# A recurrent and windowed-attention network on one core: another order of work around the exponentials, zero rows stored in turns, gated weights loaded in parts

## The reference, cut to what matters

```
h = shift_token(x)                       # second half of the columns from the token before
q, k, v = split(h @ wqkv)                # 8 heads of 64
q, k = rotary_xpos(l2norm(q) * qs, l2norm(k) * ksc)
o = softmax(mask(8 * q @ k.T)) @ v       # windows of 128 tokens, each sees itself and the one before
x = x + o @ wo
h = layernorm(shift_token(x)) * lg + lb
a, g = split(h @ w1 + b1)                # 2 x 682
x = x + (a * gelu(g)) @ w2 + b2
```

## Time and profile before

| | |
|---|---|
| median of 3 runs | 6583.36 us |
| the profiled execution | 6587.74 us, its span 6585.7 us |
| TensorE matmul | 5333.4 us busy (81%) |
| VectorE | 4306.0 us (65%) |
| GpSimd | 3300.1 us (50%) |
| ScalarE | 2826.9 us (43%) |
| first attention | about 1899 to 3103 us of the span |
| first gated stage | about 3103 to 3709 us |
| second attention | about 3709 to 4889 us |
| second gated stage | about 4889 to 5495 us |

### The profile page before, as it was taken

One profiled execution on the slowest core, in us unless ns is written; L12 is line 12 of the kernel. 1 busy time (PEld: TensorE's weight loads), 2 busy tenths in 40 slices (PEclk: granted clock), 3 DMA queues, 4 the chain that ended last, 5 costly groups with the idle time before them and its releaser, 6 DMA issues. The chain is left out here.

```text
span 6585.7 us, 79275 instructions
## 1 busy us (share of the span) xinstructions
PE 5333.4 (81%) x26028; PEld 3102.2 (47%) x26028; DVE 4306.0 (65%) x8780; ACT 2826.9 (43%) x6006; POOL 3300.1 (50%) x1922
## 2 busy tenths in 40 slices
PE   6777777777648888887999888888869998996878
PEld 2222222222226666665555466666645554554755
DVE  5999999999956666665333366666643334663349
ACT  5776767767624444443111244444431112331233
POOL 5989898999944334442001233443320103776424
PEclk8888888788769999998999999999989999998988
DMA  5555555555530111111111110011111114443856
GB/s 121 128 126 128 120 129 122 137 119 131 120 107 30 33 30 30 30 31 41 44 39 48 44 32 30 30 30 33 30 40 48 39 45 153 131 135 85 224 172 196
DMA packets 501100, 549.85 MB, mean 83 GB/s; under 512 B 71749, under 2 KB 401349, under 8 KB 496596
## 3 DMA queue, kind: packets, MB, share of 16 engines
q1 hardware_dynamic: 463460, 522.79, 29.2%
q10 hardware_dynamic: 9584, 19.80, 0.9%
q0 software_dynamic: 27648, 2.19, 0.4%
HBM read 395.60 MB, written 218.35 MB: 93 GB/s over the span
## 5 line engine op out<-in xcount | busy, mean ns | idle before, releaser
L616 POOL TENSOR_TENSOR db<-durep,brep 128x2048 f32<-128x2048 f32 x256 | 1159.8, 4531 | 176.1 <-DVE p_h L523 161.3
L1089 POOL TENSOR_TENSOR rn<-n,mhalf 128x16 f32<-128x16 f32 x128 | 374.9, 2929 | 1311.2 <-DVE n L1047 1311.2
L466 ACT ACTIVATE p_h<-dlrep,am 128x512 f32<-128x512 f32 x1024 | 703.9, 691 | 205.4 <-DVE hh L534 169.3
L321 PE MATMUL p_acc<-hh,fold 128*32 128x512 f32 x2048 | 355.2, 773 | 487.2 <-DVE hh L534 486.8
L523 DVE TENSOR_TENSOR_SCAN p_h<-p_h,hlast,db 128x512 f32<-128x512 f32 x576 | 720.7, 1284 | 0.0
L1324 POOL TENSOR_TENSOR grstd<-grstd,mhalf 128x4 f32<-128x4 f32 x32 | 32.6, 1018 | 1065.2 <-DVE grstd L1272 1065.2
L1257 ACT ACTIVATE gg<-p_g,b 114x512 f32<-114x512 f32 x192 | 132.0, 687 | 975.0 <-PE p_a L1223 974.9
L534 DVE TENSOR_TENSOR hh<-p_h,crep 128x512 f32<-128x512 f32 x768 | 520.0, 677 | 0.0
L800 PE MATMUL p_qk<-wqkv,hT 128*128 128x512 f32 x1024 | 502.6, 614 | 8.1 <-DVE rot_sin L1041 7.2
L927 ACT ACTIVATE probB<-probB,nb 128x256 f32<-128x256 f32 x512 | 253.6, 496 | 549.5 <-DVE nb L1006 549.5
L1790 POOL DMA_INDIRECT dispatched<-xe,idx x384 | 395.3, 1029 | 130.7 <-issue 113.8
(11 more groups left out here) (251 smaller groups left out, 11845.6 us busy)
## 6 DMA issues: line engine op xcount, KB each, us to landing
dlrep<-delta_rows SPq DMA_DIRECT2D x256, 256.0 KB
durep<-drive_rows SPq DMA_DIRECT2D x256, 256.0 KB
ew<-in_L_ffn_w SPq DMA_DIRECT2D x192, 176.0 KB
brep<-bc_rows SPq DMA_DIRECT2D x64, 256.0 KB
crep<-bc_rows SPq DMA_DIRECT2D x64, 256.0 KB
delta_rows<-dl SPq DMA_DIRECT2D x64, 256.0 KB
drive_rows<-du SPq DMA_DIRECT2D x64, 256.0 KB
hx<-stream SPq DMA_DIRECT2D x256, 64.0 KB, 2.0
```

The source lines that it names most:

```text
L321: ins = pe.matmul(p_acc[32 * j:32 * j + 32, :], fold[:], hh[s % 2][:, j], start=False, stop=(g == NG - 1), skip_group_check=True)
L466: act.activation(p_h[:, (i % BANKS) * CH:(i % BANKS + 1) * CH], dlrep[use % 2][:, j], ACT.Exp, scale=am[:, q, j, g:g + 1]).then_inc(s_ex, 1)
L616: pool.tensor_tensor(out=db[s % 2][:], in0=durep[use % 2][:], in1=brep[c % 2][:, g:g + 1, :].to_broadcast([P, 4, CH]), op=ALU.mult).then_i ...
L1089: pool.tensor_tensor(out=rn[k][:], in0=n2[k][:], in1=mhalf[:], op=ALU.pow).then_inc(s_rn, 1)
```

## The change

In attention:

- TensorE's order becomes: scores A, turned input, weighted values B, scores B, project, queries/keys 1, and on as before.
- ScalarE's order becomes: turned B, turned input, exps A 1 and 2, output, exps A 3 and 4, turned A, 4 exps B, squares, and on as before.
- VectorE takes the maxima of B right after the division of A, ahead of the residual.
- Each of the four maxima gives a signal of its own, and each exponential waits for its own one.
- The 16 stores of zero rows are issued one in every fourth round of the first layer, at the round's head.

In the gated stage SP loads the first activations, then `w1` in two halves, the second activations, and `w2`. ScalarE's queue loads scale and shift, `b1` and `b2`. Each load has a semaphore of its own group, and an engine waits for it at its first use.

```diff
@@ attention, TensorE: scores
-                        pe.wait_ge(s_nb[1], t)
+                        pe.wait_ge(s_nb[1], 4 * t)
                 else:
-                    pe.wait_ge(s_nb[0], t + 1)
+                    pe.wait_ge(s_nb[0], 4 * (t + 1))
@@ attention, TensorE: the round
                     scores(t, 0)
-                if t >= 1:
-                    weighted_values(t - 1, 1)
                 if f < NT:
                     turn_in(f)
                 if t >= 1:
-                    project(t - 1)
+                    weighted_values(t - 1, 1)
                 if now:
                     scores(t, 1)
+                if t >= 1:
+                    project(t - 1)
@@ attention, ScalarE: exps
-            def exps(t, half):
-                if t > 1:
+            def exps(t, half, js):
+                if js[0] == 0 and t > 1:
                     act.wait_ge(s_rden[half], t - 1)
-                act.wait_ge(s_nb[half], t + 1)
-                for j in range(4):
+                for j in js:
                     h = head_at(half, j)
+                    act.wait_ge(s_nb[half], 4 * t + j + 1)
                     ins = act.activation(prob[half][:, j], prob[half][:, j], ACT.Exp, bias=nb[:, h:h + 1], scale=-1.0,
                                          accum_out=den[t % 2][:, h:h + 1])
-                ins.then_inc(s_exp[half], 1)
+                if js[-1] == 3:
+                    ins.then_inc(s_exp[half], 1)
@@ attention, ScalarE: the round
+                if l == 0 and now and t % (NT // NZ) == 0:
+                    clear_slots(t // (NT // NZ))
                 if t >= 1:
                     turn_prob(t - 1, 1)
-                    turn_out(t - 1)
                 if f < NT:
                     turn_in(f)
                 if now:
-                    exps(t, 0)
-                    exps(t, 1)
+                    exps(t, 0, (0, 1))
+                if t >= 1:
+                    turn_out(t - 1)
+                if now:
+                    exps(t, 0, (2, 3))
                     turn_prob(t, 0)
+                    exps(t, 1, (0, 1, 2, 3))
@@ attention, VectorE: maxima, then the round
-                ins.then_inc(s_nb[half], 1)
+                    ins.then_inc(s_nb[half], 1)
...
                     normalise(t, 0)
+                    maxima(t, 1)
                 if t >= 1:
                     residual(t - 1)
                 if now:
-                    maxima(t, 1)
@@ gated, SP
-            sp.dma_start(w1[:], A["L0_ffn_w1"][l].rearrange("(c p) n -> p c n", p=P)).then_inc(s_w, 16)
...
+            load_h(0)
+            for f in range(DH):
+                sp.dma_start(w1[:, f], A["L0_ffn_w1"][l, f * P:(f + 1) * P, :]).then_inc(s_w1l, 16)
+            load_h(1)
             for j in range(NJ):
                 n = BLK[j]
-                sp.dma_start(w2[0:n, j, :], A["L0_ffn_w2"][l, j * BJ:j * BJ + n, :]).then_inc(s_w, 16)
...
+                sp.dma_start(w2[0:n, j, :], A["L0_ffn_w2"][l, j * BJ:j * BJ + n, :]).then_inc(s_w2l, 16)
@@ gated, ScalarE
-            act.wait_ge(s_w, 16 * GLOADS)
+            for q, nm in enumerate(("L0_ffn_ln_g", "L0_ffn_ln_b")):
+                v = A[nm][l].unsqueeze(1)
+                for f in range(DH):
+                    act.dma_start(lgb[:, q, f:f + 1], v[f * P:(f + 1) * P, :]).then_inc(s_ln, 16)
+            b1f = A["L0_ffn_b1"][l].unsqueeze(1)
+            for j in range(NJ):
+                for q in (1, 0):
+                    n, at = BLK[j], q * HID + j * BJ
+                    act.dma_start(b1[0:n, q, j:j + 1], b1f[at:at + n, :]).then_inc(s_b1l, 16)
+            act.dma_start(b2[:], A["L0_ffn_b2"][l:l + 1, :].to_broadcast([P, D])).then_inc(s_b2l, 16)
+            act.wait_ge(s_b1l, 32 * NJ)
```

More of the change, by code:

```diff
@@ L955, in values, with clear_slots @@
                 act.activation(vv[f % RING][:], p_v[:], ACT.Copy).then_inc(s_ve, 1)
[L957 to L961, removed]
+            def clear_slots(n):
+                if n == 0:
+                    act.wait_ge(s_zeros, 1)
+                act.dma_start(xb_d[n * ZR * P:(n + 1) * ZR * P, :].rearrange("(p r) e -> p (r e)", r=ZR),
+                              slot_zeros[:]).then_inc(s_zeroed, 16)
             for t in range(-2, NT + 1):
                 now, f = 0 <= t < NT, t + 2
+                if l == 0 and now and t % (NT // NZ) == 0:
+                    clear_slots(t // (NT // NZ))
                 if t >= 1:
                     turn_prob(t - 1, 1)
-                    turn_out(t - 1)
                 if f < NT:
@@ L1092, in _ @@
                 if f >= RING:
-                    pool.wait_ge(s_nb[1], f - RING + 1)
+                    pool.wait_ge(s_nb[1], 4 * (f - RING + 1))
                 pool.wait_ge(s_rn, f + 1)
@@ L1159, in gated @@
     p_y = ps("p_y", CT * D)
-    s_w = sem("g_weights")
+    s_w1l, s_w2l, s_b1l, s_ln, s_b2l = (sem("g_" + n) for n in ("w1_loads", "w2_loads", "b1_loads", "ln_loads", "b2_load"))
     s_h, s_r, s_out = ([sem(f"g_{n}{k}") for k in range(2)] for n in ("h", "r", "out"))
@@ L1175, in load_h @@
                                  tiles(rows(2 * l + 1, chunk_slot(c), CH, src)[:, cols])).then_inc(s_h[c % 2], 16)
-            sp.dma_start(w1[:], A["L0_ffn_w1"][l].rearrange("(c p) n -> p c n", p=P)).then_inc(s_w, 16)
-            b1f = A["L0_ffn_b1"][l].unsqueeze(1)
+            load_h(0)
+            for f in range(DH):
+                sp.dma_start(w1[:, f], A["L0_ffn_w1"][l, f * P:(f + 1) * P, :]).then_inc(s_w1l, 16)
+            load_h(1)
             for j in range(NJ):
                 n = BLK[j]
-                sp.dma_start(w2[0:n, j, :], A["L0_ffn_w2"][l, j * BJ:j * BJ + n, :]).then_inc(s_w, 16)
[L1182 to L1191, removed]
+                sp.dma_start(w2[0:n, j, :], A["L0_ffn_w2"][l, j * BJ:j * BJ + n, :]).then_inc(s_w2l, 16)
             for c in range(NC):
@@ L1217, in up @@
                 if j == 0:
+                    if c == 0:
+                        pe.wait_ge(s_w1l, 16 * DH)
                     pe.wait_ge(s_hT, c + 1)
@@ L1227, in down @@
             def down(c):
+                if c == 0:
+                    pe.wait_ge(s_w2l, 16 * NJ)
                 pe.wait_ge(s_hid, NJ * (c + 1))
@@ L1237, in down @@
                     ins.then_inc(s_w2, 1)
-            pe.wait_ge(s_w, 16 * GLOADS)
             turn(0)
@@ L1303, in residual @@
                                   op=ALU.add).then_inc(s_y, 1)
-            dve.wait_ge(s_w, 16 * GLOADS)
             prepare(0)
+            dve.wait_ge(s_ln, 32 * DH)
             turn(0)
+            dve.wait_ge(s_b1l, 32 * NJ)
             for c in range(NC):
@@ L1324, in rsqrt @@
                 pool.tensor_tensor(out=rstd[:], in0=rstd[:], in1=mhalf[:, 0:CT], op=ALU.pow).then_inc(s_rs, 1)
-            pool.wait_ge(s_w, 16 * GLOADS)
             rsqrt(0)
+            pool.wait_ge(s_b2l, 16)
             for c in range(NC):
@@ L1333, in _ @@
                                    op=ALU.add).then_inc(s_rb, 1)
-GLOADS = 1 + 3 * NJ + 2 * DH + 1
 def route(nc, ctx, A, rows, x_in, ssm_out, xb_d, x1_d, xn1_d, xt_d, y_d, odd_d, kv_d, ident, mhalf, zrow):
```

## The result

The changed kernel takes 6308.44 us (median of 4 runs, 6303.65 to 6311.38), the one before 6584.01: a ratio of 0.958, 95% interval 0.9564 to 0.9597. Forecast were 6315 and a range of 6278 to 6410.

A forecast was written before the change was run, and what follows sets the result against it. TensorE was the nearest bound, with holes from waits. Gains of 220 (tiles), 23 (zero rows) and 25 (gated loads) sum to 268 us: 6319.7 from the profiled 6587.7, 6315 against the median; range 6278 to 6410.

The forecast's parts named there:

- The wait before the turning of queries and keys: TensorE in attention: 1.57 us a tile waiting for ScalarE's copy of the turned probabilities, forecast to go.
- The division A as what is late next: VectorE in attention: division A, running against GpSimd, ends 6.97 us after the power, at 8.07; the turning of A follows.
- The period: Attention tile: from 17.85 to 16.11 us, steady gain 1.75 us in 126 tiles, 220 us.
- The last tile of each layer: Attention: the gain needs a full neighbouring tile, so 63 of a layer's 64 tiles were counted.
- The signals, priced at nothing: Attention: signals on each maximum and waits on each exponential cost 0, upper end 0.4 us a tile or 50 us.
- The second rival: Attention: division A's last quarter also waits for GpSimd's table product; period 16.85, gain 126 us, time 6409; chance 0.14.
- Zero rows: Start of the first attention: without sixteen stores ahead of the loads, first scores come 22.8 us sooner; spread stores are hidden.
- Gated loads: Start of both gated stages: activations loaded before weights move the chain forward 12.5 us each, 25 in all.
- by the division and by TensorE's own queue alike: TensorE in attention: the turning of A starts at 8.17 us after the scores A, held by both.
- the first rival: Attention: TensorE alone decides, small waits vanish; period 15.9 to 15.8, gain 252 us, time 6283; chance 0.12.
- The slower rival: Attention: division A waits for GpSimd and its four parts hold GpSimd back; period 19.0, time 6679; chance 0.05.
- the one in which only the beginnings gain: Attention: all four division parts wait until GpSimd is through; loop stays 17.85, time 6535; chance 0.05.

The follow-up runs named there:

- the first experiment: Kernel before with one edit, ScalarE copying the turned A ahead of the exponentials B: 6488.7 us, ratio 0.9857.
- the second: Kernel before with only TensorE's order changed (turned input, weighted values B, scores B, projection): 6589.1 us, ratio 1.001.
- two experiments: Kernel after with one signal for four maxima, 6381.0 us; kernel before with only the turned A ahead of the exponentials B, 6488.7 us.
- the extra product: Kernel after with one more GpSimd product (1.04 us, into a scratch tile) between power and sum of each tile: 6451.0 us, ratio 0.9802.
- the experiment: Kernel after, but four maxima give one signal and an exponential waits for all four of its half: 6381.0 us, ratio 0.9694.
- the two experiments with the norms first: Kernel after with norms ahead of VectorE's rotation products, 6250.5 us; that kernel with exponentials B ahead of the turned A again, 6230.6 us.

## Why the prediction was right, step by step

- **The wait before the turning of queries and keys** goes because ScalarE copies the turned A first: shown by the first experiment, where it is gone, and by the second, where it stays.
- **The division A as what is late next, its end read from the second layer's first tile** (6.97 us after the power): 6.98 in the timeline after. The same pattern of collisions came back with the same start, 4.13 against 4.10; where the start was later, 5.10 and 5.39 in two experiments, the end was later too, 7.57 and 7.86. It was the step that carried the size, and the extra product shows that it is the bound: 143 us.
- **The period** was forecast at 16.1 and is 16.06; that, 0.05 x 126, is 6 us. The last tile of each layer, which I left out, gives another 3 us in each (21.1 from its scores to the next stage after, 24.3 before). Together they are the 12 of 14 us by which the tile loops gave more than the 220 forecast: 141.1 + 116.1 - 22.8 = 234.4.
- **The signals, priced at nothing**, cost nothing: the maxima still follow each other at 0.41 us. What they gain was in the schedule (exponentials from 2.1); the experiment puts it at 73 us. Without them the division starts 1 us later and the table product catches it, which is shown for 17 of the 73, and the projection is late as well. The second rival's trigger was thus real, and missed by less than 1 us.
- **Zero rows** 22.8 us forecast and 22.8 in the trace, 21 by the run. The issues took 0.33 to 0.36 us each where I had 1.06, and were hidden. **Gated loads** 25 forecast, 25.0 in the windows, 20 by the run, within its interval. The windows are no finer than that: the same gated stage of before took 605.6 us in one kernel's trace and 602.1 in another's. The load that I called the first half of the weights, 1.4 MB, is both halves; `w1` has 256 x 1364 numbers of 4 bytes, so one half is 0.7 MB. Nothing in the sum hung on it.
- **One step was mis-sized**: that the turning of A is held "by the division and by TensorE's own queue alike". By its queue TensorE was ready 7.83 us after the scores A (projection at 4.28, then 1.83 and 1.72) and not at 8.17; the turning started at 8.14 because of the division alone. The sum came out right because the division's end was right; that the queue was forecast 0.3 us too late did no harm beside it.
- **The terms that were too long** in that queue are lengths read from the old order. The projection takes 1.92 us to the next item where the scores B stand behind it, and 1.83 in the new order, where the queries do; the queries take 1.82 behind the scores B and 1.72 behind the projection or the turning of A. In every kernel here with the old order of TensorE the projection is 1.92 and the queries never under 1.82; in every one with the new order they are 1.83 and, where nothing is waited for, 1.72. It is no wait for the division: in the kernel with TensorE's order undone the 1.82 are there too, and its division has ended at least 1.2 us before the turning of A starts. The weight loads of the kernel before, beside the earlier trace rows, put the extra time into the first of the four matmuls of the queries:

```profile
2604.11 0.19 PEld L800 LDWEIGHTS p_qk<-wqkv,hT 128*128 128x128 f32 x1 [0.24 <-issue]
2604.54 0.19 PEld L800 LDWEIGHTS p_qk<-wqkv,hT 128*128 128x128 f32 x1 [0.24 <-issue]
2605.11 1.08 PEld L855 LDWEIGHTS p_t<-ident,probA 128*128 128x128 f32 x8 [0.38 <-issue]
```

From 2603.58 to 2604.11 it is 0.53 us, from there to the next 0.43. Why the first is longer behind the scores, no run shows. So TensorE's new order also shortens its own work, by 1.92 + 1.82 - 1.83 - 1.72 = 0.19 us a tile, which pays only where TensorE is the bound. TensorE alone needs 15.6 us a tile, not 15.8 to 15.9, and the two experiments with the norms first took 0.35 and 0.5 us a tile of what I had written off: with them the first rival (TensorE alone) comes true, at a shorter period than it had.

- **The slower rival** did not come, nor did the one in which only the beginnings gain. The loop that they rest on is there (the extra product goes round it in full), but only as many collisions as in the earlier trace rows. That the division also holds GpSimd back is seen once a tile: GpSimd's small scaling takes 0.38 us beside it and 0.24 away from it.

The parts are not additive. Turned A first gives 95 us, TensorE's order nothing; without TensorE's order the rest is slower than before by 1.8%, the fallen clock included.

## What to carry to other kernels

When a wait goes, work out what is late next, and look for a place in the old trace where that thing already happens in the new alignment: here the first tile of a layer showed it. An idle engine isn't free to load: what counts is what it collides with, and when. Orders of several engines are one edit; judge them together. An item's length can depend on what stands before and behind it, so read it, where you can, in the new order's neighbourhood.

## What the runs showed that was not expected

- With a gap of 2.0 us in TensorE's work in every tile, of 18 to 20 us, the granted clock fell to the lower level for some 3 us behind part of the gaps (0.94 over the window); the 33 of 51 tiles in which it fell were 1.6 us longer than the rest. In the kernel before, with gaps of 1.6 us in a period of 17.85, it stayed at 1.00.
- The same items of TensorE took 0.1 us more or less by what stood next to them: queries 1.82 or 1.72 us, projection 1.92 or 1.83.
- VectorE's division of one half took 1.14 us where GpSimd stood still, and 1.37, 1.65, 1.95, 2.47, 2.85 or 4.02 us in these runs with GpSimd's instructions beside it; the four instructions themselves were the same.
- A store of zero rows took ScalarE's queue 1.06 us each in a burst of sixteen and 0.33 when spread.
